# A graph-attention and expert-layer kernel: its last phase spread over TensorE, GpSimd and ScalarE, and part of a scatter moved forward

## The reference, cut to what matters

```
x      = layernorm(x)                                   # 12500 nodes x 256
x      = x + graph_mix(x)                               # neighbour sums, linear layers: the stages before the last
x2     = layernorm(x)
h      = x2 @ W_gat                                     # 4 heads x 4 experts, edges: 131072 + one loop per node
e      = leaky_relu(a_src[src] + a_dst[dst])
agg    = softmax over the edges of each node, sum of h[src] * alpha
scores = layernorm(agg) averaged over the heads         # 4 scores for each node
top 2 of the 4 experts, w = softmax(their two scores), g[e] = w of expert e, else 0
out    = x + sum over e of g[e] * (gelu(x2 @ W1[e] + b1[e]) @ W2[e] + b2[e])
```

## Time and profile before

| | us |
|---|---|
| median of 3 runs | 4135.55 (4126.72 to 4138.9) |
| the profiled execution, its own time | 4134.59 |
| its span | 4132.8 |

### The profile page before, as it was taken

The page is one execution under the profiler, slowest core; times in us unless marked ns, Lnnn a source line. Parts: engine busy times, 40 slices in busy tenths (PEclk is TensorE's granted clock), DMA queues, the critical chain, the costliest instruction groups (busy, mean ns, idle before and its releaser), DMA issues. The chain is left out here.

```text
span 4132.8 us, 46229 instructions
## 1 busy us (share of the span) xinstructions
PE 3223.6 (78%) x12938; PEld 2165.0 (52%) x12938; DVE 2084.5 (50%) x4892; ACT 801.7 (19%) x1966; POOL 2856.3 (69%) x2937
## 2 busy tenths in 40 slices
PE   0599899998987888887887799999899999991000
PEld 0355556665655655555555466666666666661000
DVE  6577777776765866665554212223222322312888
ACT  6122222222200111111111122222122221220000
POOL 2677777777777777777775577777777777775610
PEclk6799999999998999999998899999999999995555
DMA  8555555554545666667666222222222222223787
GB/s 260 177 134 134 133 134 135 135 136 132 137 135 137 174 175 173 175 172 202 175 174 157 62 71 64 60 69 77 64 64 58 74 69 66 63 55 92 214 259 256
DMA packets 381412, 540.56 MB, mean 131 GB/s; under 512 B 120314, under 2 KB 297818, under 8 KB 381143
## 3 DMA queue, kind: packets, MB, share of 16 engines
q0 software_dynamic: 119136, 234.44, 25.0%
q1 hardware_dynamic: 243119, 288.12, 21.7%
q10 hardware_dynamic: 19016, 16.48, 1.2%
HBM read 392.03 MB, written 146.74 MB: 130 GB/s over the span
## 5 line engine op out<-in xcount | busy, mean ns | idle before, releaser
L787 POOL DMA_INDIRECT rows<-xn_rows,gsrc x1664 | 1611.1, 968 | 509.8 <-issue 509.2
L1357 POOL DMA_INDIRECT nb<-route_rows,idx x1024 | 1015.9, 992 | 321.8 <-issue 303.1
L1088 PE MATMUL PS<-rows,oh 128*128 128x257 f32 x3328 | 876.0, 412 | 264.6 <-DMA rows<-xn_rows,gsrc 263.2
L1088 PEld LDWEIGHTS PS<-rows,oh 128*128 128x128 f32 x3328 | 646.2, 203 | 412.2 <-DMA rows<-xn_rows,gsrc 303.6
L1690 PE MATMUL PS<-arena,hid 128*125 128x256 f32 x3200 | 700.5, 381 | 29.2 <-ACT hid L1649 20.9
L1682 PE MATMUL PS<-x2g,arena 128*128 128x500 f32 x1600 | 680.1, 586 | 23.5 <-DMA x2g<-x_turned 13.4
L1690 PEld LDWEIGHTS PS<-arena,hid 128*125 128x125 f32 x3200 | 601.0, 188 | 138.8 <-issue 33.1
L1621 DVE TENSOR_TENSOR y_sb<-PS,b_b 125x512 f32<-125x512 f32 x200 | 128.5, 684 | 1041.0 <-PE PS L1690 1040.9
L1682 PEld LDWEIGHTS PS<-x2g,arena 128*128 128x128 f32 x1600 | 305.8, 191 | 383.5 <-issue 357.7
L1649 ACT ACTIVATE hid<-PS,b_sb 128x500 f32<-128x500 f32 x400 | 270.5, 677 | 673.0 <-PE PS L1682 672.8
L824 DVE TENSOR_TENSOR oh<-PS,rel 128x1024 f32<-128x1024 f32 x208 | 253.9, 1221 | 9.2 <-issue 1.0
(11 more groups left out here) (304 smaller groups left out, 3083.9 us busy)
## 6 DMA issues: line engine op xcount, KB each, us to landing
y_rows<-y_sb SPq DMA_DIRECT2D x100, 512.0 KB, 2.7
arena<-y_rows SPq DMA_DIRECT2D x100, 512.0 KB, 5.7
rows<-xn_rows,gsrc POOLq DMA_INDIRECT x1664, 3.4
nb<-route_rows,idx POOLq DMA_INDIRECT x1024, 2.4
sum_rows<-kept SPq DMA_DIRECT2D x104, 128.5 KB
x_rows<-x SPq DMA_DIRECT2D x100, 128.0 KB, 4.7
hid<-x_rows SPq DMA_DIRECT2D x100, 128.0 KB, 6.8
m_in<-sum_rows SPq DMA_DIRECT2D x100, 125.5 KB
```

The source lines that it names most:

```text
L787: pool.indirect_dma_start(out=rows[w][h][:, q, 0:D], out_offset=None, in_=xn_rows, in_offset=bass.IndirectOffsetOnAxis(ap=gsrc[:, s * HU + ...
L1088: last = mm(SUM[:, 0:D + 1], oh[w][h][:, q, :], rows[w][h][:, q, :], start=h == 0 and q == 0, stop=h == 1 and q == HU - 1)
L1357: pool.indirect_dma_start(out=nb[b % NBUF][:, c, :], out_offset=None, in_=route_rows, in_offset=bass.IndirectOffsetOnAxis(ap=idx[:, b * W ...
```

## The change

- The first 42 tiles' scatters to `ad_rows` are issued by GpSimd at the end of the graph stage, after its last row gather (`SOONER`), the other 58 where they were.
- `unit_after` gives other tiles: before 12, 20, 24, 32, 36, 41, 48, 53, 60, 65, 72, 76, 84, 88, 96, 100 for the 16 batches, now 9, 16, 21, 28, 33, 40, 45, 52, 57, 64, 69, 76, 81, 88, 93, 100.
- Two "own" loads are issued before the first load of results, the three others behind the last batch's records. They go to storage of their own in the freed `nb` buffers, as the result gathers do, so neither waits for an earlier `weigh`. There are YR = 12 buffers for tiles.
- The gates are made in six parts (4, 16, 20, 20, 20, 20 tiles) instead of five blocks, at places of a list (`PLAN`). The list has tiles 0 to 39 first, then tiles 60 to 99 two to one among tiles 40 to 59.
- Tiles 0 to 59 are read in full. The odd 30 of them are summed by TensorE: ScalarE makes four diagonal matrices from the gates, TensorE multiplies them with the four results and adds x by the identity, ScalarE copies the sum to the accumulator.
- For tiles 60 to 99 VectorE also finds the two experts of rank 0 and 1 (`pick`), GpSimd gathers those two rows of 1 KB for every node (two indirect DMAs a tile), ScalarE issues the load of x, and VectorE sums with two operations. There are GR = 5 buffers for it.
- Many semaphores are merged (`s_lane`, `s_turns`, `s_weigh`, `s_roots` and others), with no other waits by it.

```diff
-YR = 8
+YR = 12
 AR = 4
 FT = 20
+PARTS = ((0, 4), (4, 20), (20, 40), (40, 60), (60, 80), (80, 100))
+GR = 5
+CHOSEN = 40
+CHOSEN_AT = 40
+WEIGHED_AT = (0, 0, 12, 20, 28, 36)
+BY_PE = 30
+SOONER = 42
...
-    t = int((b + 1) * 5.8) + 7
+    t = 6 * (b + 1) + 3
     return t if t % 4 < 2 else t + 4 - t % 4
...
+def final_plan():
+    read = NT - CHOSEN
+    by_pe = lambda t: (t * BY_PE) // read != ((t + 1) * BY_PE) // read
+    plan, t, chosen = [], 0, 0
+    for n in range(NT):
+        plan += [("weigh", k) for k, at in enumerate(WEIGHED_AT) if at == n]
+        if n >= CHOSEN_AT and (t == read or chosen * (NT - CHOSEN_AT) <= CHOSEN * (n - CHOSEN_AT)) and chosen < CHOSEN:
+            plan.append(("chosen", read + chosen))
+            chosen += 1
+        else:
+            plan.append(("turned" if by_pe(t) else "read", t))
+            t += 1
+    return plan
...
+                pool.wait_ge(s_adz, RH * 16)
+                pool.wait_ge(s_hc, SOONER + 1)
+                for t in range(SOONER):
+                    pool.indirect_dma_start(out=ad_rows, out_offset=bass.IndirectOffsetOnAxis(ap=start_i[:, t:t + 1], axis=0),
+                                            in_=ad_all[:, t, :], in_offset=None).then_inc(s_ads, 16)
...
+                for k in range(2):
+                    load_own(k)
                 sp.wait_ge(s_y, NT)
                 for u in range(2):
                     sp.wait_ge(s_ys[u], 16 * NT // 2)
-                for t in range(YR):
-                    final_loads(t)
+                for i in range(YR):
+                    final_loads(i)
                 for b in LATE:
                     store_records(b)
-                for t in range(YR, NT):
-                    final_loads(t)
+                sp.wait_ge(s_rec, NB - 1)
+                sp.wait_ge(s_own, 32)
+                for k in range(2, FG):
+                    load_own(k)
+                for i in range(YR, len(BY_READ)):
+                    final_loads(i)
...
-                for t in range(NT):
+                for t in range(SOONER, NT):
                     pool.indirect_dma_start(out=ad_rows, out_offset=bass.IndirectOffsetOnAxis(ap=start_i[:, t:t + 1], axis=0),
...
+                for i, t in enumerate(BY_CHOICE):
+                    pool.wait_ge(s_fix, PICKED.index(part_of(t)) + 3)
+                    if i >= GR:
+                        pool.wait_ge(s_acc, BY_DVE.index(BY_CHOICE[i - GR]) + 1)
+                    for c in range(2):
+                        pool.indirect_dma_start(out=three[i % GR][:, c * D:(c + 1) * D], out_offset=None, in_=y_by_expert,
+                                                in_offset=bass.IndirectOffsetOnAxis(ap=pick_i[:, c, t:t + 1], axis=0)).then_inc(s_two[i % GR], 16)
...
+                def combine_chosen(t):
+                    n, i = PLACE[t], BY_CHOICE.index(t)
+                    q = i % GR
+                    dve.wait_ge(s_two[q], (i // GR + 1) * 32)
+                    dve.wait_ge(s_third[i % 2], (i // 2 + 1) * 16)
+                    if n >= AR:
+                        dve.wait_ge(s_out[n % AR], (n // AR) * 32)
+                    for c in range(2):
+                        if c:
+                            v.drain()
+                        last = v.scalar_tensor_tensor(out=acc[n % AR][:], in0=three[q][0:NP, c * D:(c + 1) * D], scalar=two_gates[:, c, t:t + 1],
+                                                      in1=acc[n % AR][:] if c else three[q][0:NP, 2 * D:3 * D], op0=ALU.mult, op1=ALU.add)
+                    last.then_inc(s_acc, 1)
...
+                def third(i):
+                    if i >= 2:
+                        act.wait_ge(s_third[i % 2], i // 2 * 16)
+                    act.dma_start(three[i % GR][:, 2 * D:3 * D], x1_rows[BY_CHOICE[i]]).then_inc(s_third[i % 2], 16)
+                def diagonals(i):
+                    t = BY_TURN[i]
+                    act.wait_ge(s_weigh, 4 * part_of(t) + 4)
+                    if i >= 2:
+                        act.wait_ge(s_turned, i - 1)
+                    for e in range(NE):
+                        last = a(turn[i % 2][:, e, :], ident[0:NP, 0:NP], ACT.Copy, scale=gate[:, t, e:e + 1])
+                    last.then_inc(s_diag, 1)
+                def take_turned(t):
+                    n, i = PLACE[t], BY_TURN.index(t)
+                    act.wait_ge(s_turned, i + 1)
+                    if n >= AR:
+                        act.wait_ge(s_out[n % AR], (n // AR) * 32)
+                    a(acc[n % AR][:], TURNED[i % 2][0:NP, 0:D], ACT.Copy).then_inc(s_turnedc, 1)
+                    act.wait_ge(s_turnedc, i + 1)
...
+                for how, k in PLAN:
+                    if how == "weigh":
+                        roots(k)
+                        weighed += 1
+                    elif how == "turned":
+                        take_turned(k)
+                        taken += 1
+                        store_out(k)
+                    else:
+                        act.wait_ge(s_acc, BY_DVE.index(k) + 1)
+                        store_out(k)
+                        if how == "chosen" and BY_CHOICE.index(k) + GR < len(BY_CHOICE):
+                            third(BY_CHOICE.index(k) + GR)
+                    while made < len(BY_TURN) and made < taken + 2 and part_of(BY_TURN[made]) < weighed:
+                        diagonals(made)
+                        made += 1
...
+                for i, t in enumerate(BY_TURN):
+                    at = BY_READ.index(t)
+                    q = at % YR
+                    pe.wait_ge(s_diag, i + 1)
+                    pe.wait_ge(s_yl[q], (at // YR + 1) * 32)
+                    if i >= 2:
+                        pe.wait_ge(s_turnedc, i - 1)
+                    mm(TURNED[i % 2][0:NP, 0:D], ident[0:NP, 0:NP], x1_in[q][0:NP, :], start=True, stop=False)
+                    for e in range(NE):
+                        last = mm(TURNED[i % 2][0:NP, 0:D], turn[i % 2][:, e, :], y_in[q][0:NP, e * D:(e + 1) * D], start=False, stop=e == NE - 1)
+                    last.then_inc(s_turned, 1)
```

More of the change, by code:

```diff
@@ L150, in unit_after, with part_of @@
 def unit_after(b):
-    t = int((b + 1) * 5.8) + 7
+    t = 6 * (b + 1) + 3
     return t if t % 4 < 2 else t + 4 - t % 4
+def part_of(t):
+    return [lo <= t < hi for lo, hi in PARTS].index(True)
+def final_plan():
[11 more added lines that the diff above has]
+    return plan
+PLAN = final_plan()
+FINAL = [item for item in PLAN if item[0] != "weigh"]
+PLACE = {t: n for n, (_, t) in enumerate(FINAL)}
+BY_READ = [t for how, t in FINAL if how != "chosen"]
+BY_DVE = [t for how, t in FINAL if how != "turned"]
+BY_CHOICE = [t for how, t in FINAL if how == "chosen"]
+PICKED = sorted({part_of(t) for t in BY_CHOICE})
+BY_TURN = [t for how, t in FINAL if how == "turned"]
 def build(nc, x, src, dst, gnn_w, gnn_b, wqkv, wkv_t, wout_t, bout, w_gat, att_src, att_dst,
@@ L1227, in build @@
             z4, d4 = one("z4", [P, 3, RH]), one("d4", [P, 2, RH])
-            own, res = two("own", [NP, FT, ROW]), two("res", [P, FT, REC])
+            own = two("own", [NP, FT, ROW]) + [nb[2][0:NP, k * FT:(k + 1) * FT, :] for k in range(FG - 2)]
+            as_records = nb[0][:].rearrange("p w c -> p (w c)")[:, 0:(FG - 2) * FT * REC].rearrange("p (k t c) -> p k t c", k=FG - 2, t=FT)
+            res = two("res", [P, FT, REC]) + [as_records[:, k, :, :] for k in range(FG - 2)]
             zf, df = one("zf", [NP, 3, FT, RH]), one("df", [NP, 2, FT, RH])
@@ L1278, in build @@
             s_yl = [ev(f"s_yl{q}") for q in range(YR)]
+            s_two = [ev(f"s_two{q}") for q in range(GR)]
+            s_third = [ev(f"s_third{u}") for u in range(2)]
+            s_diag = ev("s_diag")
+            s_turned = ev("s_turned")
+            s_turnedc = ev("s_turnedc")
             s_acc = ev("s_acc")
             s_out = [ev(f"s_out{q}") for q in range(AR)]
+            ends_in = lambda k: sum(PARTS[j][1] - PARTS[j][0] for j in range(k % 2, k + 1, 2))
             batches_after = lambda t: [b for b in range(NB) if unit_after(b) == t]
@@ L1515, in first_records @@
                     v.drain()
-                    v.tensor_tensor(fix[:, 0:20], fix[:, 0:20], back[:, 1, :], ALU.add).then_inc(s_fixed, 1)
-                def weigh(k):
[L1520 to L1526, removed]
+                    v.tensor_tensor(fix[:, 0:20], fix[:, 0:20], back[:, 1, :], ALU.add).then_inc(s_fix, 1)
@@ new lines, in weigh @@
+                def weigh(k):
+                    first, end = PARTS[k]
+                    m, of_block = end - first, slice(first % FT, first % FT + end - first)
+                    ow, rs = own[first // FT][0:NP, of_block, :], res[first // FT][0:NP, of_block, :]
+                    bc = lambda a: a[:].rearrange("p (o c) -> p o c", o=1).broadcast_to([NP, m, 16])
+                    zf_k, df_k, q5_k, q6_k, rden_k, agg_k, asq_k = zf[:, :, 0:m, :], df[:, :, 0:m, :], q5[:, 0:m, :], q6[:, 0:m, :], rden[:, 0:m, :], agg[:, 0:m, :], asq[:, 0:m, :]
```

(19 more changed lines are left out.)

254 lines of the change are left out of this document (146 added, 108 removed).

## The result

| | before | after |
|---|---|---|
| median, same chip | 4131.14 us (4126.29 to 4138.90, 4 runs) | 4079.36 us (4078.49 to 4080.03, 4 runs) |
| ratio | | 0.9873, 95% interval 0.9854 to 0.9892 |
| span of the profiled execution | 4132.8 us | 4078.1 us |
| first tile summed by VectorE | 3842.94 | 3802.47 |
| from there to the end | 289.9 | 275.6 |

The kernel is faster by 1.3%. The profiled executions differ by 54.7 us, of which 40.5 come ahead of the first sum and 14.2 behind it; the forecast had 39 to 41 and 43.

What follows compares the result with a forecast made beforehand. GpSimd's queue was taken to bound the kernel up to 3773.7 us, VectorE from there. First sum at 3802, plus 131 + 110 + 5, gave 4048, and with 1.8 around the span 4050 us; range 4005 to 4095.

Steps and rivals of the forecast that it cites:

- The front: Everything ahead of VectorE's first tile sum: 39 to 41 us of the 85 to be gained.
- the last part: From VectorE's first tile sum to the end: 43 us to be gained, 131 + 110 + 5 = 246 us.
- a sign of being wrong: Stated test of the forecast: a last part over 275 us or under 215, or first result gather after 3775.
- Start of the last stage: 42 scatters move into GpSimd's idle 57.8 us, 53.6 us earlier; last batch lands at 3723 instead of 3773.7.
- Expert layers: Scoring at hand-set tiles leaves TensorE's outputs no waits; TensorE done 24.5 us earlier, last tile's copy at 3709.
- The handover: Last records land at 3752, first result gather 3761 instead of 3800, first VectorE sum 3802 against 3842.9.
- The 11 us that I charged for the queue: Last records stand behind own and paired loads on SyncE's queue, landing 11 us later than on a free queue.
- The first 40 tiles: Start of the last part: weighings and picks 72 us, bursts of sums 19 + 3 x 12 + 4, sum 131.
- 5 to land: Output stores: 5 us for a store to land and free its accumulator, used in pricing the bursts.
- The last 60 tiles: End of the last part: accumulators set 1.8 us a slot, 108, taken as 110, plus 5 for the last store.
- DMA binds: Rival: at 210 GB/s the last part takes 283 us, 4087 us in all; chance 0.16.
- Only engines bind: Rival: stores land in time, last part 114 + 97 + 8 us, 4023 us in all; chance 0.22.

Runs made afterwards that it cites:

- e5: Changed kernel with all 100 scatters back in the last stage, none early: 4132.54 us, ratio 0.9987 to the kernel before.
- e4: Changed kernel with the last batch's records stored ahead of the 12 pairs of loads: 4078.50 us, ratio 0.9851 to the kernel before.
- e9: Changed kernel with three edits (empty rows spread, eight accumulators, last records stored ahead of the loads): 4032.47 us, ratio 0.9762 to the kernel before.
- e6: Changed kernel with empty rows spread and eight accumulators instead of four: 4048.59 us, ratio 0.9781 to the kernel before.
- e1: Changed kernel with an empty row of its own for each node of a tile: 4065.93 us, ratio 0.9825 to the kernel before.
- e3: Changed kernel with eight accumulators instead of four, the one empty row left: 4064.81 us, ratio 0.982 to the kernel before.
- e2: The kernel before with only the empty rows spread: 4127.59 us, ratio 0.9975 to the kernel before.
- e11: e9 with VectorE summing all 60 read tiles, none by TensorE: 4050.02 us, ratio 0.980 to the kernel before.
- e10: e9 with no tile gathered, all 100 read in full, 30 summed by TensorE: 4031.92 us, ratio 0.9765 to the kernel before.

## Why the prediction was right, and where it fell short

The direction and the range held; the gain was 52 us where I had 85. The front gave the 40 that I had, the last part 14 instead of 43. Its 275.6 us are just over the 275 that I had named as a sign of being wrong, so the sum for the last part must be called wrong, though the time lies in the range.

- **Start of the last stage: held.** 42 x 1.275 = 53.6 us forecast for the last landing's shift; the scatters start at 2251.2, and the last batch is scored at 3719.37 against 3723. Some luck is in it. The first neighbour gather starts at 2386.93, not 2381, and the gathers then take 8 us less than before, which I hadn't forecast. "Fits with 4 to spare" was a little off too: from the last row gather to the opening of the last stage it takes 60.5 to 61.1 us in the eleven runs with early scatters and 58.0 to 58.7 in the three without. In all eleven the stage opens 6.04 us after the last scatter's end, which points to GpSimd as the engine that now comes last. e5 puts the worth of the scatters at 47 to 49 us.
- **Expert layers: held.** No wait for neighbours' rows but the last, the last copy at 3712.49 against 3709 (the stage opened some 5 us later in this execution). That the hand-set tiles were needed for it was argued; undoing them alone wasn't tried.
- **The handover: held.** Records landed at 3751.9 against 3752, first result gather 3761.27 against 3761, first sum 3802.47 against 3802. The 11 us that I charged for the queue are 9 in e4 and 10.6 in e9 against e6, each the balance of a gain of 13 to 14 and a loss of some 4. By the rule of one ring served in order (DMA: Bandwidth & Descriptors of the Trainium skill, section Queues, rings and completion order), the trace agrees.
- **The first 40 tiles: the step that failed** (four bursts of sums between weighings, paced by four accumulators). "Sum 72 + 19 + 3 x 12 + 4 = 131" measured 165.6. The bursts were under by 25: some 12 of it is the one empty row, by e1. The rest is "5 to land" for a store, right for a quiet moment and too short beside the loads: in e1 the bursts are still 72. The weighings were under by 9, for I kept ScalarE's functions at their old price although I gave ScalarE diagonals, copies and stores in the same list.
- **The last 60 tiles: the number held, not its reason.** 110 against 110 and 5. I had the accumulators set the pace; eight of them change it by 2 us (e3). (1.0 + 0.3 + 0.8 + 5 is 7.1, not 7.2; it changes nothing.)
- **The rival "DMA binds"** came closer in time, 4087, partly by luck: the last part moved its bytes at 219 GB/s, near the 210 of that rival, but at a DMA share of 0.76, so the engines were not full for all of it. I had the evidence of the slow stretch in hand: the window of 210 GB/s at a share of 0.89. I put the slowness down to an "own" load, which had been issued ahead of 3870, over thirty us earlier. The view of the queues for that window shows GpSimd's queue with 30.6% of the engines' time for 0.14 MB. "Against it: the result gathers end by 3890" was the wrong way round: they end at 3890, and up to there they did the harm. That packing them together costs more than the two groups of the kernel before fits 15.4 us (e1) against 10 (e2).
- **"Only engines bind"** is refuted for this kernel: it had the last part at 219 us, and even with the three edits e9 takes 240.8.

What the change brought, then: the early scatters 47 of its 52 us. Sums by TensorE and gathers of chosen rows, most of its code, gave 4 us each in the last part when they were undone one at a time, and nothing that the ratios show; undoing both together wasn't tried. Half a screen of edits (e9) gives 46 more by the ratios (0.9762 / 0.9873) and makes TensorE's part worth 18.

## What to carry to other kernels

A DMA share near 1 with few GB/s is a question, not an answer: look at the queues' own shares in that window, and at the addresses. A gather whose padding all points at one row can be slow for every queue, as it was here; give it as many rows as there are lanes. (How slow a gather is that is padded in part no run here shows.) And before an engine gets more work, see which list it stands in: here ScalarE's exponential waited behind stores, and the 19 us that the weighings grew ate half of the 40 that TensorE had freed in the bursts (e11 against e9).

## What the runs showed of the hardware that was not expected

- Gathers that all read the same 96-byte row of HBM: 0.52 us of a DMA engine for a packet of some 400 bytes, against 0.023 to 0.030 where the rows differ. Two loads of 512 KB that SyncE issued while such gathers ran, from 3880 to 3890, landed after 17.7 us, against a median of 6.0 in the window from 3806 to 3828.
- With slow DMA engines the issue itself blocks: two stores 5.91 us instead of 0.8 on ScalarE, which stands still for it; with the empty rows spread (e1) the longest in the same stretch took 1.12 us.
- The DMA engines moved 382 GB/s from 3806 to 3828 with loads of 4 KB and 1 KB pieces and stores of 1 KB or less side by side, at a share that the profile gives as 1.03; e10 holds 367 for 113 us. 338 was the most I had read in the rows of before.
